# A norm moved to ScalarE, a band's mask to GpSimd, and the keys streamed once in a fused attention block

## What is computed

```
# 1. a non-local block: three 1x1 projections, softmax over one axis of 128, projection back
attn = softmax(theta @ phi, axis=1);  x = w_mask(attn @ g) + x
# 2. tokens t (256 per unit, 128 channels); banded attention with two window sizes on the normalised tokens
z = layernorm(t);  q, k, v = z @ qkv_w.T, 8 heads of 16
for ws in (9, 17):                       # |i - j| <= ws // 2, that is 4 and 8
    out += softmax(where(band, q k^T / 4, -max)) @ v
t = t + (out / 2) @ proj_w.T + proj_b
# 3. a quantised dense layer on the normalised tokens
t = t + qdq_e4m3(layernorm(t)) @ qdq_e4m3(kernel) + bias
```

## Time and profile before

| | |
|---|---|
| median of three runs | 106.75 us (106.66 to 107.17) |
| the profiled execution | 106.25 us |
| its span, first to last instruction | 104.5 us |
| mean granted TensorE clock | 0.907 |
| busy: PE, DVE, ACT, POOL | 87.1, 77.4, 63.5, 56.3 us |
| DMA moved | 2.90 MB, mean 28 GB/s |

### The profile page before, as it was taken

One profiled execution on the slowest core, in us unless ns is written; L12 is line 12 of the kernel. 1 busy time (PEld: TensorE's weight loads), 2 busy tenths in 40 slices (PEclk: granted clock), 3 DMA queues, 4 the chain that ended last, 5 costly groups with the idle time before them and its releaser, 6 DMA issues.

```text
span 104.5 us, 4371 instructions
## 1 busy us (share of the span) xinstructions
PE 87.1 (83%) x1825; PEld 65.7 (63%) x1825; DVE 77.4 (74%) x283; ACT 63.5 (61%) x174; POOL 56.3 (54%) x118
## 2 busy tenths in 40 slices
PE   0799786999997999999999999989979757777260
PEld 0485474877775888797688788658849536444120
DVE  0011528199999999999999999999999895736221
ACT  1524556679584649974967956994996644162520
POOL 6810202057593944939799296789649464630300
PEclk9999999999999999999999999999999975555555
DMA  0725400000000000000010010000101010010101
GB/s 22 205 49 170 157 0 0 6 0 0 9 3 0 9 0 6 0 6 0 6 56 0 0 56 3 6 6 0 50 6 56 0 55 5 6 50 0 50 0 50
DMA packets 3971, 2.90 MB, mean 28 GB/s; under 512 B 944, under 2 KB 3952, under 8 KB 3952
## 3 DMA queue, kind: packets, MB, share of 16 engines
q1 hardware_dynamic: 3728, 2.56, 7.8%
q10 hardware_dynamic: 224, 0.07, 0.3%
HBM read 1.57 MB, written 1.05 MB: 25 GB/s over the span
## 4 chain that ended last, share of the span: by engine, by line
PE 55%; DVE 27%; POOL 8%; issue 3%; ACT 2%; DMA 2%; DVEq 0%
PE bank L309 10%; PE bank L323 5%; PE bank L331 5%; PE bank L300 4%; PE bank L257 4%; PE bank L266 4%; PE bank L252 4%; PE bank L274 3%; DVE row_max L791 3%; PE bank L293 3%; DVE z_sb L780 3%; PE bank L289 3%; DMA phi_w<-in_L_conv_w_phi_dram 2%; PE bank L272 2%; PE bank L294 2%
## 5 line engine op out<-in xcount | busy, mean ns | idle before, releaser
L309 PE MATMUL bank<-k_pad,q_four 64*64 64x64 f32 x512 | 17.4, 220 | 1.2 <-ACT q_four L548 1.1
L309 PEld LDWEIGHTS bank<-k_pad,q_four 64*64 64x64 f32 x512 | 15.8, 135 | 3.1 <-ACT q_four L548 1.8
L1122 POOL TENSOR_TENSOR prob<-expd,row_inv 128x256 f32<-128x256 f32 x16 | 9.9, 616 | 9.8 <-DVE row_inv L806 9.8
L323 PEld LDWEIGHTS bank<-prob_t,v_win 32*32 32x32 f32 x1024 | 10.9, 110 | 5.2 <-issue 2.7
L1116 POOL TENSOR_TENSOR diff<-narrow,row_max 128x192 f32<-128x192 f32 x16 | 8.2, 514 | 10.3 <-DVE row_max L791 10.3
L323 PE MATMUL bank<-prob_t,v_win 32*32 32x32 f32 x1024 | 12.7, 199 | 1.0 <-DVE prob_t L810 1.0
L548 ACT ACTIVATE q_four<-bank,four_mask 128x256 f32<-128x256 f32 x32 | 12.6, 483 | 0.0
L791 DVE TENSOR_REDUCE row_max<-bank 128x16 f32<-128x512 f32 x16 | 10.7, 671 | 2.1 <-ACT narrow L555 2.1
L1097 POOL TENSOR_TENSOR rstd<-ve,minus_half 128x2 f32<-128x2 f32 x8 | 5.6, 701 | 11.9 <-DVE ve L774 11.8
L555 ACT COPY narrow<-bank 128x192 f32<-128x192 f32 x16 | 5.1, 318 | 8.0 <-PE bank L309 8.0
L1129 POOL TENSOR_TENSOR prob<-prob,narrow_prob 128x192 f32<-128x192 f32 x16 | 9.5, 594 | 0.5
(11 more groups left out here) (116 smaller groups left out, 213.2 us busy)
## 6 DMA issues: line engine op xcount, KB each, us to landing
x_all<-in_x_dram SPq DMA_DIRECT2D x8, 128.0 KB, 3.8
out_dram<-out_all SPq DMA_DIRECT2D x8, 128.0 KB, 1.7
qkv_rows<-in_L_attn_qkv_w_dram SPq DMA_DIRECT2D x1, 192.0 KB, 2.6
proj_rows<-in_L_attn_proj_w_dram SPq DMA_DIRECT2D x1, 64.0 KB, 2.7
ffn_k<-in_L_ffn_kernel_dram SPq DMA_DIRECT2D x1, 64.0 KB, 2.2
proj_bias<-in_L_attn_proj_b_dram SPq DMA_DIRECT2D x1, 64.0 KB, 4.4
theta_w<-in_L_conv_w_theta_dram SPq DMA_DIRECT2D x1, 32.0 KB, 2.0
phi_w<-in_L_conv_w_phi_dram ACTq DMA_DIRECT2D x1, 32.0 KB, 2.4
```

Source lines behind the costliest of these rows:

```text
L309: last = mm(ps_scores[g][q, w, :, :], q_four[q, u % SLOTS, g * WB + w, :, :].rearrange("p e q -> p (e q)"), k_pad[q, u % SLOTS, at:at + KW ...
L323: last = mm(ps_pv[q, at:at + QUAD], v_win[q, u % SLOTS, g * WB + w, :], prob_t[q, u % SLOTS, g, w, :], start=True, stop=True)
L1122: p.tensor_tensor(prob[:, u % SLOTS, g], wide_part(expd, u, g), row_inv[:, u % SLOTS, g, 0].unsqueeze(2).to_broadcast([C, WB, KW]), ALU.mult)
```

## The change

Four things change.

- The scores of a window are streamed once. A bank holds 8 times 32 columns, under the wide mask alone (`key_mask` loses its `KINDS` dimension). The narrow mask, 24 columns, the same for every window, is spread once over the partitions by a matmul (`spread_narrow`) and kept in SBUF (`keep_narrow_mask`).
- The narrow band is made from the wide one: `copy_narrow` copies its 8 by 24 columns to `near`, the new `mask_narrow` (POOL) adds the narrow mask, the new `narrow_max` (DVE) takes the maximum, and `subtract_narrow` waits for that. `band_max` reduces 256 columns and not 512.
- `norm_first` leaves DVE. `variance_first` makes one more small product, `lift1` = minus the mean; `rstd_first` (POOL) makes `slope1` from it, with 1/sigma and -mean/sigma; ACT writes z as slope times the PSUM bank plus offset.
- The five lists of calls are in a new order.

```diff
-        ps_scores = [bank[4 + g][:, :].rearrange("p (w k n) -> p w k n", w=WB, k=KINDS) for g in range(BANKS)]
+        ps_scores = [bank[4 + g][:, 0:WB * KW].rearrange("p (w n) -> p w n", w=WB) for g in range(BANKS)]
...
+            def spread_narrow():
+                pe.wait_ge(masks_made, 1)
+                pe.wait_ge(weight_done, 3)
+                mm(bank[6][:, C:C + NW], query_sel[:, :, :].rearrange("p h q -> p (h q)"), narrow_rows[:, :],
+                   start=True, stop=True).then_inc(weight_mm, 1)
...
-                mm(bank[4 + g][:, :], query_sel[:, :, :].rearrange("p h q -> p (h q)"),
-                   key_mask[:, g:g + WB, :, :].rearrange("p w k n -> p (w k n)"), start=True, stop=False)
+                mm(bank[4 + g][:, 0:WB * KW], query_sel[:, :, :].rearrange("p h q -> p (h q)"),
+                   key_mask[:, g:g + WB, :].rearrange("p w n -> p (w n)"), start=True, stop=False)
...
-                        last = mm(ps_scores[g][q, w, :, :],
+                        last = mm(ps_scores[g][q, w, :],
                                   q_four[q, u % SLOTS, g * WB + w, :, :].rearrange("p e q -> p (e q)"),
-                                  k_pad[q, u % SLOTS, at:at + KW].unsqueeze(1).to_broadcast([SIDE, KINDS, KW]),
+                                  k_pad[q, u % SLOTS, at:at + KW],
...
+            def keep_narrow_mask():
+                act.wait_ge(weight_mm, 5)
+                nc.scalar.copy(narrow_mask[:, :], bank[6][:, C:C + NW]).then_inc(mask_kept, 1)
...
+            def norm_first(u):
+                act.wait_ge(slope1_done, u + 1)
+                for s in range(2):
+                    last = nc.scalar.activation(z_sb[:, u, halves(s)], ps_t[:, halves(s)], ACT.Identity,
+                                                scale=slope1[:, u, 0, s:s + 1], bias=slope1[:, u, 1, s:s + 1])
+                last.then_inc(z_done, 1)
...
-                nc.scalar.copy(narrow[:, u % SLOTS, g], ps_scores[g][:, :, 1, INSET:INSET + NW]).then_inc(narrow_kept[g], 1)
+                nc.scalar.copy(near[:, u % SLOTS, g], ps_scores[g][:, :, INSET:INSET + NW]).then_inc(narrow_kept[g], 1)
...
-            def norm_first(u):
-                dve.wait_ge(t_kept, u + 1)
-                dve.wait_ge(rstd1_done, u + 1)
-                for s in range(2):
-                    last = v.tensor_scalar(z_sb[:, u, halves(s)], ps_t[:, halves(s)], mv1[:, u, s, 0:1],
-                                           rstd1[:, u, s:s + 1], ALU.subtract, ALU.mult)
-                last.then_inc(z_done, 1)
+                v.tensor_tensor(lift1[:, u, 1, :], mv1[:, u, :, 0], minus_one[:, :], ALU.mult).then_inc(var1, 1)
...
-                v.tensor_reduce(row_max[:, u % SLOTS, g], ps_scores[g], AX.X, ALU.max).then_inc(max_done[g], 1)
+                v.tensor_reduce(row_max[:, u % SLOTS, g, 0], ps_scores[g], AX.X, ALU.max).then_inc(max_done[g], 1)
...
+            def narrow_max(u, g):
+                dve.wait_ge(narrow_made[g], u + 1)
+                v.tensor_reduce(row_max[:, u % SLOTS, g, 1], narrow[:, u % SLOTS, g], AX.X, ALU.max).then_inc(nmax_made[g], 1)
...
-                pool.wait_ge(var1, u + 1)
+                pool.wait_ge(var1, 2 * (u + 1))
                 p.tensor_tensor(rstd1[:, u, :], ve1[:, u, :], minus_half[:, :], ALU.pow).then_inc(rstd1_done, 1)
+                pool.wait_ge(rstd1_done, u + 1)
+                p.tensor_tensor(slope1[:, u], lift1[:, u], rstd1[:, u, :].unsqueeze(1).to_broadcast([HALF, 2, 2]),
+                                ALU.mult).then_inc(slope1_done, 1)
...
+            def mask_narrow(u, g):
+                if u == 0:
+                    pool.wait_ge(mask_kept, 1)
+                pool.wait_ge(narrow_kept[g], u + 1)
+                p.tensor_tensor(narrow[:, u % SLOTS, g], near[:, u % SLOTS, g],
+                                narrow_mask[:, :].unsqueeze(1).to_broadcast([C, WB, NW]), ALU.add).then_inc(narrow_made[g], 1)
```

582 lines of the change are left out of this document (315 added, 267 removed).

## The result

The changed kernel took **109.88 us** (median of four runs, 108.79 to 110.92) against 106.85 for the kernel before on the same chip: ratio 1.025, interval 1.016 to 1.034. It is slower by 3 us where 2.4 us less was forecast. Its profiled execution took 109.5 us, span 107.8, which is 3.3 above the span before.

A forecast was written before the change was run, and what follows sets the result against it. VectorE was taken to bound a 65 us plateau, between a ramp and a tail bound by chains. Terms +2.1 +0.8 -2.6 -4.1 +0.6 +1.4 +0.9 -1.5 sum to -2.4 us: median 104.4 us, forecast 102.6 to 106.1, range 102.0 to 107.9.

The forecast's parts named there:

- a plateau of 65 us, bound by DVE: From 20.8 to 86.0 us: VectorE, busy 98%, was taken to set the pace, so work taken off it would save time.
- PE does not bound the plateau: In the plateau: savings on TensorE were hidden by VectorE's work, worth at most some 0.5 us in the ramp; value taken 0.
- the term of -4.1 for z: In the plateau, units 2 to 7: the first norm's z leaves VectorE, where it was busy 0.69 us a unit; -4.1 us.
- -2.6 for the quantisation: In the plateau: quantise_parts moves ahead of the first band_max, into a wait of VectorE; -2.6 us.
- Behind pick_odd(7) nothing changes: End of the tail: after pick_odd(7) the times stay as before, 0 us.
- The ramp: Up to the first scores: costlier z's and copy_kq(0) queued behind z(1) make scores start 2.1 us later, at about 21.35.
- The rival by the Trainium skill: Score matmuls: loads and streams follow one another within a row group, so half the stream shortens scores; 103.6 us, chance 0.08.
- The tail's middle: From pick_odd(6) to pick_odd(7): 6.3 us in place of 7.9, taken as -1.5 us.
- The slower rival: Small two-input operations of both norms: VectorE waits on GpSimd, 0.35 us a pair; 108.2 us if all wait; chance 0.24.
- the +0.9: Small two-input VectorE operations out of SBUF: more stalls until GpSimd lets go, +0.9 us.
- the 2.8 of the sum: VectorE's idle time in the plateau: 1.4 us before, doubled in the forecast, a term of +1.4 us.
- the 4 that I had named as the sign of being wrong: The plateau: VectorE idle above 4 us, whoever ends it, would show the forecast wrong.

The follow-up runs named there:

- e11: The kernel before with the matmul of the values issued twice from unit 2 on, 0.43 us more TensorE work a unit; 108.85 us against 106.45 without.
- e12: The kernel before with one row sum done twice from unit 2 on, 0.41 us more VectorE work a unit; 108.33 us against 106.45 without.
- e4: The kernel before with only quantise_parts moved ahead of the first band_max on VectorE; 105.67 us, ratio 0.994.
- e14: The changed kernel with z of the first norm made by VectorE again, other orders as in the change; 111.18 us.
- e10: The changed kernel with one row sum done twice from unit 2 on, 0.41 us more VectorE work a unit; 110.14 us.
- e3: The changed kernel with GpSimd masking the narrow band of only one window in eight; 108.65 us.
- e1: The changed kernel with masks of 512 columns and keys streamed twice again; 108.95 us, ratio 1.027.
- e9: The changed kernel with the matmul of the values issued twice from unit 2 on, 0.43 us more TensorE work a unit; 110.42 us.
- e16: The changed kernel with turn_z2(6) ahead of project(7) and unread filler matmuls ahead of TensorE's waiting calls at the end; 113.43 us.
- e17: The changed kernel with variance_second(7) ahead of result(6) on VectorE and norm_second(7) ahead of add_bias(7) on ScalarE; 109.49 us.
- e8: The changed kernel with copy_kq(0) ahead of z of unit 1 (norm_first(1)) on ScalarE; 117.15 us.
- e15: The kernel before with quantise_parts moved ahead of the first band_max and unread filler matmuls ahead of TensorE's waiting calls at the end; 106.92 us.

## Why the prediction was wrong

**The step that failed** is in its first part: "a plateau of 65 us, bound by DVE", and from it "PE does not bound the plateau" and the term of -4.1 for z, -2.6 for the quantisation, less what came in their place. The busy share of 98% was read as the bound, and TensorE's own busy share, 94% in the same row, was waved off because its ends are modelled. The idle time of TensorE in the plateau was not asked for. It was 1.9 us of 53.6, and, if its records are taken as they stand, that is the most that a lighter VectorE could bring there. e11 and e12 settle which engine set the pace: in the steps from unit 2 to unit 5 it was TensorE alone, and VectorE's work counted in the first step and in the last two. So the terms had to shrink to what those steps give: e4 got 0.8 of the 2.6, e14 puts the move of z at 2 at most of the 4.1, and the change got 0.3 in all.

**The clock** was the second. The tail's lower clock was in the sum as it stood; that its start might move was not. Where it fell while the last scores still ran, the stretch from unit 7's scores to `pick_odd(6)` is long: 9.4 us in the change (fall at 81.1), 9.9 in e10 (81.0) and 10.0 in e3 (80.7). Where it held past `pick_odd(6)`, it is 7.8 in e1 and 7.9 in e9. That stretch in the change, in e10 and in e9:

```profile
81.10:89.40 8.30, 7.53 (x175) 5.57 (x172) 6.68 (x25) 3.60 (x10) 5.75 (x12) 0.50 0.02 5
```
```profile
80.50:90.38 9.88, 8.93 (x205) 6.96 (x204) 8.20 (x31) 4.86 (x13) 6.57 (x14) 0.53 0.08 26
```
```profile
83.11:91.02 7.91, 5.77 (x205) 4.53 (x204) 7.70 (x29) 4.76 (x13) 6.53 (x14) 1.00 0.08 22
```

The same 205 records are 8.93 us of TensorE at the one level and 5.77 at the other. So of the +2.1 in this piece about 1.5 is the clock, by an estimate from 9.4 us against the 7.8 and 7.9 of e1 and e9. Why it falls earlier in the change stays open: in e1, with the old stream, it fell at 89.8, but in e9, with the thin one and two records a unit more, it fell once at 28.6 and then not until 93.5. Ahead of the fall TensorE had been busy 4.31 of 5.10 us in the change (76.0 to 81.1), 3.79 of 5.00 in e10 (76 to 81) and 4.31 of 5.70 in e16 (78.0 to 83.7); in e9 13.42 of 17.50 us (76.0 to 93.5) went by at 1.00, so that a busy share alone does not tell them apart. The change's four runs took 108.79, 109.5, 110.26 and 110.92 us at mean clocks of 0.886, 0.876, 0.871 and 0.868.

**"Behind pick_odd(7) nothing changes"** was the third, +1.3. Unit 6 stood 3.8 us later than before at `pick_odd(6)` and 3.2 at its `result`, unit 7 2.0 at `pick_odd(7)`, since only unit 7 had been pulled forward, and `result(6)` (99.90) is ahead of `variance_second(7)` (100.30) on VectorE, with `aggregate_second(7)` done at 99.13. e17 shows it for 0.7 of the 1.3; the other 0.6 is open.

**What held.** The ramp: +2.0 at unit 1's scores, by the chain that was forecast, though not its size alone. The profiles of e11 and e12, whose ramp is that of the kernel before, have that mark at 25.5 instead of 24.8. In the profile before, `mix_tokens(0)` and `column_attention(1)`, at 10 us on TensorE, took 0.60 and 0.62 us where those of e12 and of the change took 1.06 each. Against e12 the ramp is 1.3 longer, so that up to 0.7 of the agreement is luck. Timeline after, ScalarE and VectorE:

```profile
18.69 0.81 ACT L561 ACTIVATE z_sb<-bank,slope 128x128 f32<-128x128 f32 x2 [0.44 <-POOL slope L1145]
...
19.64 1.59 ACT L575 ACTIVATE q_four<-bank,four_mask 128x256 f32<-128x256 f32 x4
...
22.79 0.42 DVE L820 TENSOR_REDUCE row_max<-bank 128x8 f32<-128x256 f32 x1 [1.66 <-ACT near L582]
```

z(1), `copy_kq(0)` behind it to 21.2, scores at 21.27 (21.35 forecast), the first `band_max` at 22.79 (22.9). The quantisation took 1.2 us there, from 19.14. The sizes of the new operations, by groups:

```profile
L324 PEld LDWEIGHTS bank<-k_pad,q_four 64*64 64x64 f32 x512 | 16.6, 140 | 2.3 <-ACT q_four L575 1.2 <-issue 0.8
...
L820 DVE TENSOR_REDUCE row_max<-bank 128x8 f32<-128x256 f32 x16 | 6.6, 410 | 2.4 <-ACT near L582 2.4
...
L561 ACT ACTIVATE z_sb<-bank,slope 128x128 f32<-128x128 f32 x16 | 6.5, 465 | 0.8 <-POOL slope L1145 0.8
L830 DVE TENSOR_REDUCE row_max<-narrow 128x8 f32<-128x192 f32 x16 | 5.3, 338 | 0.5 <-POOL narrow L1167 0.2
```

The score loads took 140 ns (135 before), and a unit's scores 2.06 us with half the stream (2.08 before). The rival by the Trainium skill (TensorE: Matmul & The Clock Gate, Part 3, The mechanism: a load overlaps running matmuls only where the row group differs) had 0.5 us to give in the ramp; the trace does not bear it out, no part of it came. The maxima are 0.75 a bank together, 0.74 forecast. z is 0.81 a pair (0.88). DVE, ACT and POOL are busy 73.6, 68.3 and 66.0 us (72, 70.5 and 66 forecast). The tail's middle is 6.2 us (6.3).

**The slower rival** was right in sign and wrong in place. Of the small two-input operations three waited on GpSimd (0.47, 0.55 and 0.57 us), as three did before, so neither the +0.9 nor the rival's price came. The three began within 0.06 us of the start of one of GpSimd's instructions and ended with it; ten of the other thirteen began while GpSimd had none under way, for all its 85%. A busy share was again the wrong measure. VectorE was idle 7.1 us between its first `band_max` and `pick_odd(6)`, more than the 2.8 of the sum and than the 4 that I had named as the sign of being wrong; 4.4 us of its waits there ended with TensorE, 0.2 with GpSimd.

## What to carry to other kernels

Two engines above 90% are two candidates: before an operation is moved off the busier, read how long the other stands idle in the same stretch, and count on no more than that. A few tenths of a microsecond added to one engine at a time in each unit, without touching the order, tells in one run each which of them sets the pace, if the times are compared unit by unit: the sum over the stage hides the steps in which the bound changes. And in a chain at the end, a gain for the last unit is kept only as far as the unit ahead of it in the in-order queues has also moved.

## What was not expected of the hardware

The granted clock could stay down through work without a gap. In e8 it fell at 22.3 after TensorE had been busy 1.52 of 4.30 us, and was 0.50 for 17.1 us in which it was busy 16.51; in e16 it was low from 83.7 to 90.6, busy 6.90 of 6.90 us. In e15, with filler matmuls through every wait of the tail, it stayed at 1.00 for the last 18 us, where in e4 it was at 0.50 from 85.3 on; a pair of 128x128 f32 turnings is 0.38 us at the one level and 0.69 at the other.

A score matmul that streams 32 columns against 64 columns of f32 weights takes as long as one that streams 64: 2.06 and 2.08 us for a unit's 64 records, 0.03 us a record. And a single pair of calls in another order in the first 20 us (e8) moved the time by 7 us: what the ramp loses is kept to the end.
